# Region attention with a depthwise convolution: index words read four at once, values stored in two DMAs a row, and x, residual and output rows moved by DMAs that POOL begins

## The reference

```
xn = group_norm(x)                      # 32 groups, statistics over a whole image
q, k, v = split(xn @ qkv_w.T + qkv_b)   # 1x1 convolution
q_r, k_r = mean of q, k over each of 7 x 7 regions of 8 x 8 positions
idx = top_k(q_r @ k_r, 4)               # for each of 49 regions the 4 most similar ones
out = softmax(q * 256**-0.5 @ k[idx].T) @ v[idx]   # 8 heads of 32, 64 queries x 256 keys a region
out = out + depthwise_conv3x3(v, lepe_w) + lepe_b
result = x + out @ out_w.T + out_b
```

## Time and profile before

| | us |
|---|---|
| median of 3 runs | 2189.56 (2187.88 to 2190.34) |
| profiled execution, its own time | 2192.58 |
| its span, first to last instruction | 2190.8 |
| PE busy | 1837.4 (84%) |
| DVE busy | 1661.0 (76%) |
| ACT busy | 1623.5 (74%) |
| POOL busy | 617.6 (28%) |
| granted TensorE clock, mean | 0.973 of full |

### The profile page before, as it was taken

How to read it: one execution, slowest core, us unless ns; L and a number is a source line. 1 busy time by engine, 2 the same in 40 slices (tenths; PEclk the granted TensorE clock), 3 DMA queues, 4 the chain that set the end, 5 groups by cost and what they waited for, 6 DMA issues and landing times.

```text
span 2190.8 us, 80869 instructions
## 1 busy us (share of the span) xinstructions
PE 1837.4 (84%) x25672; PEld 1200.2 (55%) x25672; DVE 1661.0 (76%) x3843; ACT 1623.5 (74%) x5017; POOL 617.6 (28%) x1920
## 2 busy tenths in 40 slices
PE   5778888898888888898888998888888988867776
PEld 3345555565555555565556655555555555545444
DVE  4678878788887878788887888878887877766544
ACT  2448878687887787788787878777887877766664
POOL 0013323232332232333232323322323232323222
PEclk9999999999999999999999999999999999998998
DMA  3213333333333333333333333333333333322323
GB/s 108 60 58 89 99 107 99 101 99 111 101 109 95 110 99 107 101 104 101 107 100 105 97 111 101 107 94 109 99 101 92 88 92 92 95 84 83 90 81 86
DMA packets 221330, 212.07 MB, mean 97 GB/s; under 512 B 19328, under 2 KB 220656, under 8 KB 220912
## 3 DMA queue, kind: packets, MB, share of 16 engines
q1 hardware_dynamic: 220912, 206.90, 33.0%
HBM read 155.45 MB, written 51.38 MB: 94 GB/s over the span
## 4 chain that ended last, share of the span: by engine, by line
SPq 69%; issue 15%; PE 8%; DMA 4%; DVE 2%; ACT 1%; POOLq 0%; POOL 0%; DVEq 0%
SPq L242 51%; SPq L210 10%; PE chunk_bank L766 4%; SPq L232 4%; DMA v_sel<-v_dram 2%; DMA v_dram<-v_stage 1%; SPq L254 1%; DVE lepe L522 1%; PE pt_bank L843 1%; SPq L259 1%; PE o_bank L857 1%; PE chunk_bank L779 1%; PE chunk_bank L755 1%; SPq L223 1%; DMA x_in<-x_dram 1%
## 5 line engine op out<-in xcount | busy, mean ns | idle before, releaser
L433 ACT ACTIVATE probs<-s_bank,neg_max 128x256 f32<-128x256 f32 x1568 | 733.6, 476 | 200.4 <-DVE neg_max L626 196.3
L313 POOL COPY k_sel<-k_all 128x128 f32 x1568 | 427.0, 307 | 1048.7 <-PE s_bank L832 1038.4
L626 DVE TENSOR_REDUCE neg_max<-s_bank 128x2 f32<-128x512 f32 x784 | 506.3, 686 | 206.7 <-PE s_bank L832 205.2
L522 DVE SCALAR_TENSOR_TENSOR lepe<-v_band,taps,lepe 128x448 f32<-128x448 f32 x896 | 612.6, 700 | 23.0 <-POOL v_band L329 13.7
L440 ACT COPY probs_t<-pt_bank 128x512 f32<-128x512 f32 x784 | 464.4, 592 | 196.7 <-PE pt_bank L843 193.5
L766 PE MATMUL chunk_bank<-xn,wqkv 128*128 128x448 f32 x1344 | 594.8, 552 | 15.0 <-ACT q_all L416 5.1
L843 PE MATMUL pt_bank<-ident,probs 128*128 128x128 f32 x3136 | 500.8, 283 | 14.3 <-ACT probs_t L440 13.0
L857 PE MATMUL o_bank<-probs_t,v_sel 128*32 128x64 f32 x12544 | 263.9, 226 | 256.9 <-DMA v_sel<-v_dram 256.0
L843 PEld LDWEIGHTS pt_bank<-ident,probs 128*128 128x128 f32 x3136 | 366.7, 143 | 157.3 <-issue 98.1
L857 PEld LDWEIGHTS o_bank<-probs_t,v_sel 128*32 128x32 f32 x12544 | 199.0, 112 | 430.8 <-DMA v_sel<-v_dram 403.1
L433 ACT ACTIVATION_READ_ACCUMULATOR probs<-s_bank,neg_max 128x1 f32 x1568 | 318.9, 203 | 0.0
(11 more groups left out here) (56 smaller groups left out, 1254.2 us busy)
## 6 DMA issues: line engine op xcount, KB each, us to landing
v_sel<-v_dram SPq DMA_DIRECT2D x1568, 64.0 KB
x_in<-x_dram SPq DMA_DIRECT2D x56, 448.0 KB, 3.9
v_dram<-v_stage SPq DMA_DIRECT2D x224, 112.0 KB
resid<-x_dram SPq DMA_DIRECT2D x56, 448.0 KB, 4.0
out_dram<-resid SPq DMA_DIRECT2D x56, 448.0 KB, 3.3
wqkv<-w_qkv_dram SPq DMA_DIRECT2D x1, 768.0 KB, 5.4
wout<-w_out_dram SPq DMA_DIRECT2D x1, 256.0 KB, 6.2
idx_row<-packed_idx SPq DMA_DIRECT2D x8, 0.2 KB
```

The costliest lines, as they stand in the source:

```text
L313: last = pool.tensor_copy(k_sel[:, r % K_SLOTS, :, RT * j:RT * (j + 1)], k_all[:, b % 2, :, bass.ds(reg[j] * RT, RT)])
L433: act.activation(probs[:, u, :], s_bank[:, u, 0:KEYS], ACT.Exp, bias=neg_max[:, r % 2, u:u + 1], accum_out=denom[:, r % 2, u:u + 1]).then_ ...
L522: ins = dve.scalar_tensor_tensor(row, v_band[:, n % BANDS, k, t // 3:t // 3 + RS, t % 3:t % 3 + W], taps[:, k, t:t + 1], row, ALU.mult, AL ...
L626: dve.tensor_reduce(neg_max[:, r % 2, 2 * hf:2 * hf + 2], s_bank[:, 2 * hf:2 * hf + 2, 0:KEYS], AX.X, ALU.max, negate=True).then_inc(max_d ...
```

## The change

- An index row now holds four 32-bit words a region. `chosen` loads all four with one call, and the shifts and masks are gone, on SP and on POOL. DVE no longer packs; the index DMA moves 16 bytes for each of 49 regions.
- v_stage is one buffer over both halves. `store_values(n)` runs once a row, at step 0 of the next s (in the last row of an image at step 6 as before), waits for both halves and begins two DMAs of 224 KB. One semaphore counts them, and `vt_out` waits for it.
- `load_x`, `load_resid` and `store_row` move to POOL's stream: load_x at step 2, store_row at step 4 (it was 3), load_resid at step 5, each behind `gather_keys(r + 2)` and, at steps 0 to 3, `add_bias`.
- `affinity` shares memory with `qk_mean`.

```
-            word = eng.value_load(idx_row[0:1, (r // NREG) % 2, n:n + 1])
-            return [nc.s_assert_within((word >> (IDX_BITS * j)) & (2 ** IDX_BITS - 1), 0, NREG - 1,
-                                       skip_runtime_bounds_check_because="max_index gives one of the 49 regions")
-                    for j in range(TOPK)]
+        def chosen(engine, r):
+            first = TOPK * (r % NREG)
+            return nc.values_load_multi_w_load_instructions(
+                idx_row[0:1, (r // NREG) % 2, first:first + TOPK], engines=[engine], min_val=0, max_val=NREG - 1,
+                skip_runtime_bounds_check_because="max_index gives one of the 49 regions")[1]
...
         @block.sync
-            def store_values(n, m):
+            def store_values(n):
                 b, rr = divmod(n, NWIN)
-                wait_taken(sp, "vt", n, m)
+                for m in range(2):
+                    wait_taken(sp, "vt", n, m)
+                if b >= 2 and rr == 0:
                     sp.wait_ge(attn_done, NREG * (b - 1))
                 for h in range(2):
+                    sp.dma_start(v_dram[b % 2, h:RS:2, rr * W:(rr + 1) * W, :].rearrange("q t d -> t q d"),
+                                 v_stage[PADW * h:PADW * h + W, :, :]).then_inc(v_stored, 16)
...
+                    if rc == 0 and is_row(s + A_LEAD - 1) and rr:
+                        store_values(s + A_LEAD - 1)
...
         @block.gpsimd
...
+            def load_resid(g):
+                if g >= 2:
+                    pool.wait_ge(out_stored[g % 2], 16 * (g // 2))
+                pool.dma_start(resid[:, g % 2, :, :], x_rows[g]).then_inc(resid_in[g % 2], 16)
+
+            def store_row(g):
+                wait_taken(pool, "out", g, 0)
+                wait_taken(pool, "out", g, 1)
+                pool.dma_start(out_rows[g], resid[:, g % 2, :, :]).then_inc(out_stored[g % 2], 16)
+
+            load_x(0)
+            load_x(1)
...
+                    if rc == 2 and 2 <= s + X_LEAD + 2 < ROWS:
+                        load_x(s + X_LEAD + 2)
+                    if rc == 4 and is_row(s - 2):
+                        store_row(s - 2)
+                    if rc == 5 and is_row(s):
+                        load_resid(s)
...
             def choose(b):
-                settle(dve.max_index(top_idx[:], top[:], affinity[:]))
-                for j in range(TOPK - 2, -1, -1):
-                    ins = dve.scalar_tensor_tensor(packed_idx[:, j:j + 1], word, float(2 ** IDX_BITS), ...
+                settle(dve.max(top[:], affinity))
+                dve.max_index(top_idx[:], top[:], affinity).then_inc(top_done, 1)
```

More of the change, by code:

```diff
@@ L7 @@
 U32 = mybir.dt.uint32
-I32 = mybir.dt.int32
 ALU = mybir.AluOpType
@@ L37 @@
 LAST_TAP = KC * (TAPS - 1) - KC
-IDX_BITS = 6
 V_SLOTS = 3
@@ L99, in attention_kernel @@
         v_band = sb("v_band", [P, BANDS, KC, RS + 2, PADW])
-        v_stage = sb("v_stage", [TWO, 2, 2, C])
+        v_stage = sb("v_stage", [TWO, 4, C])
         resid = sb("resid", [TT, 2, NT, C])
@@ L138, in attention_kernel @@
         x_loaded = [sem(f"x_loaded{i}") for i in range(2)]
-        v_stored = [sem(f"v_stored{i}") for i in range(2)]
+        v_stored = sem("v_stored")
         v_sel_in = [sem(f"v_sel_in{i}") for i in range(V_SLOTS)]
@@ L218, in _ @@
         def _(sp):
[L219 to L223, removed]
-            def store_values(n, m):
+            def store_values(n):
                 b, rr = divmod(n, NWIN)
-                wait_taken(sp, "vt", n, m)
-                if b >= 2 and rr == 0 and m == 1:
+                for m in range(2):
+                    wait_taken(sp, "vt", n, m)
+                if b >= 2 and rr == 0:
                     sp.wait_ge(attn_done, NREG * (b - 1))
                 for h in range(2):
-                    first = 4 * m + h
-                    sp.dma_start(v_dram[b % 2, first:first + 3:2, rr * W:(rr + 1) * W, :].rearrange("q t d -> t q d"),
-                                 v_stage[PADW * h:PADW * h + W, m, :, :]).then_inc(v_stored[m], 16)
+                    sp.dma_start(v_dram[b % 2, h:RS:2, rr * W:(rr + 1) * W, :].rearrange("q t d -> t q d"),
+                                 v_stage[PADW * h:PADW * h + W, :, :]).then_inc(v_stored, 16)
             def select_values(r):
-                reg = chosen(sp, r)
+                reg = chosen(mybir.EngineType.SP, r)
                 if r >= V_SLOTS:
@@ L248, in load_index @@
                     sp.wait_ge(k_sel_done, NREG * (b - 1))
[L249 to L261, removed]
+                sp.dma_start(idx_row[:, b % 2, :], top_idx[:, 0:TOPK]).then_inc(idx_in, 16)
             sp.dma_start(ident[:], ident_d).then_inc(weights_in, 16)
@@ L340, in add_bias, with load_x @@
                                    ALU.add).then_inc(resid_ready, 1)
+            def load_x(n):
+                if n >= 2:
+                    wait_full(pool, "x", n - 2, 1)
+                    wait_full(pool, "x", n - 2, 0)
+                pool.dma_start(x_in[:, n % 2, :, :], x_rows[n]).then_inc(x_loaded[n % 2], 16)
+            def load_resid(g):
[8 more added lines that the diff above has]
+            load_x(1)
             pool.memset(neg_half[:], -0.5).then_inc(zeros_done, 1)
@@ L404, in vt_out @@
                 if n:
-                    act.wait_ge(v_stored[m], 32 * n)
+                    act.wait_ge(v_stored, 32 * n)
                 wait_full(act, "vt", n, m)
                 bank = bank_of("vt", n, m)
-                act.copy(v_stage[:, m, :, :].rearrange("p q c -> p (q c)"), bank[0:TWO, :]).then_inc(free("vt", n, m), 1)
+                act.copy(v_stage[:, 2 * m:2 * m + 2, :].rearrange("p q c -> p (q c)"), bank[0:TWO, :]).then_inc(free("vt", n, m), 1)
             def q_out(n, k):
@@ L602, in choose @@
                     dve.wait_ge(idx_in, 16 * b)
-                settle(dve.max(top[:], affinity[:]))
-                settle(dve.max_index(top_idx[:], top[:], affinity[:]))
-                word = top_idx[:, TOPK - 1:TOPK]
-                for j in range(TOPK - 2, -1, -1):
[L607 to L613, removed]
+                settle(dve.max(top[:], affinity))
+                dve.max_index(top_idx[:], top[:], affinity).then_inc(top_done, 1)
             def out_half(g, m):
```

27 lines of the change are left out of this document (6 added, 21 removed).

## The result

| | before | after |
|---|---|---|
| median, us | 2188.72 (4 runs, 2187.83 to 2190.34) | 1942.59 (4 runs, 1938.21 to 1952.65) |
| ratio to before, 95% interval | | 0.888 [0.884, 0.892] |
| profiled execution, its own time | 2192.58 | 1938.21 |
| granted TensorE clock, mean | 0.973 | 0.990 |

The change makes the program 11.2% faster.

The account below looks back on a forecast made before the run. SP's queue was taken to bound the kernel, TensorE afterwards. Seven images save 178 us, the last 12, less 3.6: 186 off 2192.6 gives 2006, as median 2003 us; range 1945 to 2135.

Parts of the forecast that it names:

- in them TensorE stands 0.92 us for DVE's o_norm. I take that once a row: TensorE, four regions behind an image change: their o_norm wait, taken 7 times an image, gives 229.3 us an image.
- 222.8 us an image: TensorE's need without v_sel waits: six images' 1528 us less 191 us of waits, divided by six.
- (a): SP's queue: shifts and masks go, 0.51 us less a region.
- surcharge of 3%: Put on SP's sums because medians summed to 35.3 us a row against 36.4 measured.
- TensorE with DVE behind it is the bound, SP just under it: What is late next: TensorE at 32.7 us a row, above SP's 32.3.
- so nothing is added: Image change: v_sel path from the v_stage copy ends at 668.7, TensorE is ready at 669.2, no loss.
- (b): SP's queue: two stores a row instead of four, 0.95 us less a row.
- (c): SP's queue: x, resid and out leave it, 1.3 us less a row.
- g: POOL's cost to begin one transfer of 448 rows of 1 KB: taken as 1.2 us, three a row.
- Rival 2: POOL late at halo, then DVE, if g exceeds 2.65 us; g = 3.3 gives 2076 us; chance 0.12.
- Rival 3: v_sel lands later beside big transfers in another queue, so the relief comes to nothing: about 2190 us; chance 0.04.
- Rival 4: Less friction: no o_norm wait and a free load, 1949 us; counted within the forecast's range, no separate chance.

Follow-up runs that it names:

- runs with packing kept: DVE's three packing operations put back, unused: in the changed kernel 1945.23 us, 0.889; in the kernel before with only four-word loads 1993.07 us, 0.911.
- two loads of two words: Changed kernel with SP's load of four index words split into two loads of two, all used: 2263.47 us, 1.035.
- moves alone: Kernel before with only the x, residual and output rows begun by POOL: 2158.33 us, 0.987.
- words undone: Changed kernel back to one packed word a region, with shifts and masks on SP and POOL: 2147.66 us, 0.983.
- stores alone: Kernel before with only the values of a row stored by two DMAs in place of four: 2155.84 us, 0.985.
- words alone: Kernel before with only four index words in one load on SP and POOL, no packing: 1989.92 us, 0.909.
- moves undone: Changed kernel with x, residual and output rows begun by SP again: 1963.16 us, 0.897.
- stores undone: Changed kernel back to four stores of values a row: 1985.81 us, 0.908.
- pairs: Changed kernel with SP loading eight index words for two regions at a time: 1907.34 us, 0.872.
- fourth-load kernel: Kernel with eight words a load, and POOL also beginning the fourth load of selected values of a region: 1964.76 us, 0.898.

## Why the prediction was wrong in size

By its own sum the forecast for the profiled execution was 2006 us; it took 1938.2, 68 less.

| us | predicted | measured | difference |
|---|---|---|---|
| first image and the six, 7 times | 1605.1 | 1551.6 | -53.5 |
| last image | 219.5 | 205.7 | -13.8 |
| opening and tail, added | 3.6 | 2.6 | -1.0 |

**The step that failed: "in them TensorE stands 0.92 us for DVE's o_norm. I take that once a row".** It is an event of once an image. In the trace before, six of the seven waits for o_norm in the six images stand at 433, 686, 942, 1198, 1451 and 1707 us (0.60 to 0.92), one behind each image change; the seventh is of 0.38. I turned one wait, in four regions behind a change, into one a row, without asking whether the next row had it. The changed kernel's six images show 2.2 us in four of them, where I had put 42 x 0.92 = 38.6. The runs with packing kept say why it stood there. With it falls the prediction's order of the two: TensorE with DVE behind it was not the bound, SP was.

**The second: 222.8 us an image as TensorE's need.** It is span less wait, and takes for granted that TensorE does the same work in the same busy time once the waits go. It did not. Behind the stall of 3.58 us in the earlier trace rows the clock in the rows is 0.50, that is 1.2 GHz, and at the same place of the changed kernel, behind a stall of 1.44, it is 1.00 or 2.4 GHz. The stretches are the 3.4 us behind an image change, of the kernel before and after, columns as in the earlier trace rows (the clock is the third number from the end):

```profile
673.30:676.70 3.40, 3.40 (x19) 2.77 (x11) 1.79 (x5) 2.20 (x9) 0.00 (x0) 0.50 0.25 66
```

```profile
609.20:612.60 3.40, 3.40 (x49) 2.79 (x49) 2.67 (x7) 2.54 (x12) 1.10 (x2) 1.00 0.47 146
```

Summed over the six images, from the records of granted clock and of matmuls:

| kernel | TensorE busy, us | of the stretch at 1.2 GHz, us | six images, us |
|---|---|---|---|
| two loads of two words | 1352.8 | 119.5 | 1573.8 |
| moves alone | 1338.2 | 87.6 | 1499.5 |
| words undone | 1331.1 | 71.7 | 1486.4 |
| before | 1326.0 | 53.5 | 1528.0 |
| stores alone | 1321.4 | 47.8 | 1495.1 |
| words alone | 1313.0 | 32.2 | 1380.5 |
| moves undone | 1310.0 | 34.1 | 1355.0 |
| stores undone | 1303.6 | 17.7 | 1374.9 |
| after | 1295.7 | 6.2 | 1330.3 |
| pairs | 1293.3 | 2.0 | 1309.0 |

The busy time is, within 6 us, 1293 us plus 0.55 for each microsecond at the lower clock. Only the fourth-load kernel is off it: 1305.6 with none, and there TensorE waits on DVE. So when most of the 191 us of waits went, 30.3 us of busy time went too.

The sum of the waits does not set the time at the lower clock, though. The moves alone have less of them than the kernel before, 148.2 us for 191.0, and more at 1.2 GHz, 87.6 us for 53.5. What they have more of is long single stalls: 39 of over 1.5 us in the six images, for 20 before, 2 after and 1 in the pairs (1.5 is a bound of mine, to count by). Their number alone does not give it either: the moves undone have 6, and 34.1 us.

The six images then close: predicted 1375.6 = 1326.0 busy, 11.0 other idle, 38.6 for o_norm; measured 1330.3 = 1295.7 busy, 11.0 other idle, 23.6 for v_sel. The difference is -30.3 for the busy time, -38.6 for o_norm, +23.6 for the waits I had put at nothing.

**SP's region, 4.48 predicted, 4.20 measured.** (a) held: 4.67 less 0.51 is 4.16. The surcharge of 3%, 0.12 us, had no place on a region read whole from a timeline; it belonged to the row sum only. And e, the price of three more words, is a load behind a v_sel DMA of 0.82 us for 0.79, and 0.319 for 0.288 on POOL: 0.03, where I took 0.2. The two make the last image: 49 x 0.28 = 13.7 of its 13.8 us. A row of SP, summed over all its instructions and the gaps under 0.1 us between them, is 30.8 us where I had 32.3; TensorE's full-clock need is 1293 over 42, 30.8 too. 31.7 us a row came out, 0.9 above either, and the 0.9 is SP's own: beyond its 30.8 it stands 36.5 us in the six images, 25.4 of them at the six image changes and 11.1 in 31 gaps of 0.36 us that the profile puts down to nothing. The prediction's 32.3 names neither; its surcharge, 0.9 a row, happened to stand for them, and in the last image, which has no change of image, there was nothing for it to stand for. Both terms of "TensorE with DVE behind it is the bound, SP just under it" were too large by about the same amount, so mending one of them alone would have moved the forecast little.

The rule in the Trainium skill's "Runtime: NRT & Kernel Launch", section "Instruction fetch mechanics", some 200 ns for each register, does not hold for these loads from on-chip memory: measured are 0.03 us for three more words and 0.23 for four more after those. The prediction also read the median load of 0.63 us as agreeing with a floor of some 600 ns; the earlier trace rows itself has loads of 0.431, and behind an x, resid or out DMA 0.46 was the rule, so no floor of 0.6 shows here.

**The image change, "so nothing is added": roughly right as a path, wrong as a sum.** ACT's copy, SP and TensorE at one of them in the changed kernel:

```profile
597.57 0.60 ACT L401 COPY v_stage<-chunk_bank 114x512 f32<-114x512 f32 x1
```

```profile
598.57 3.31 DMA v_dram<-v_stage
...
601.97 0.47 SPq L207
```

```profile
609.16 0.65 PE L841 MATMUL o_bank<-probs_t,v_sel 128*32 128x64 f32 x32 [1.44 <-DMA v_sel<-v_dram]
...
614.66 0.65 PE L841 MATMUL o_bank<-probs_t,v_sel 128*32 128x64 f32 x32 [0.83 <-DMA v_sel<-v_dram]
```

The copy's end to the attend is 609.16 less 598.17, 11.0 us; I had 10.7. But TensorE is ready at 607.7, 9.6 behind the copy and not 11.2 as before. This is still not where most of TensorE's waits stand. The first attends behind the six changes wait 0 to 3.1 us, 5.3 together, where in the kernel before they waited 2.9 to 7.9. Some 18 of the 23.6 us for v_sel are spread over the rows between, as here, 75 us behind a change:

```profile
1349.01 0.76 PE L841 MATMUL o_bank<-probs_t,v_sel 128*32 128x64 f32 x20 [1.97 <-DMA v_sel<-v_dram]
```

That fits an SP whose row is as long as TensorE's and which has no lead: with the eight words SP gets its lead, and the same waits fall to 5.4 us. What an earlier change would be worth was not tried.

**(b) and (c)** held in size: 112 stores, 0.90 us a row left of 1.96, and nothing of the three big DMAs on SP. SP's row, summed as above, falls from 35.6 to 34.6 us with the stores alone, and to 35.1 with the moves alone, which is 1.3 less what the loads give back. In the kernel with the stores alone TensorE still waits for v_sel in the same manner, with 47.8 us at the lower clock.

**POOL: g = 1.2 us taken, 0.709 measured**, the median in the views of L315, L320 and L325. Rival 2 asked for 2.65 and stayed away: DVE's waits for v_band, at the line of halo that had the most of them, are 5.8 us in 7 times in place of 13.7 in 39. The value is nearer to SP's 0.40 than I took it, and far from the whole way of 3.9. add_bias waited 348.1 us for resid and now 4.0:

```profile
L308 POOL TENSOR_TENSOR resid<-resid,bout 112x256 f32<-112x256 f32 x224 | 165.4, 739 | 4.0 <-DMA resid<-x_dram 4.0
```

No such issue took the 3.1 us that the prediction drew from the page "SBUF — State Buffer" of the Trainium skill, section "SBUF: two separate sides", for a transfer beside a DVE operation in a two-port mode; the longest L320 is 0.90. Rival 3 (v_sel lands later beside the big transfers) is refuted by the waits of 23.6 us. Rival 4, 1949 us by my working, came nearest. It was right that the wait for o_norm goes and that the load's words are nearly free. That its 222.8 us an image lie so near the 221.7 measured is luck: of these TensorE is busy 216 and SP sets the pace. I had put it inside the forecast and yet set the range's lower end at it, as if nothing could go better than "no friction".

## What to carry to other kernels

When one queue is never idle, its row is a plain sum: price it region by region from a timeline, add no surcharge to it, and expect the parts of a change to add. A need worked out as span less waits contains the slow clock that stood beside the waits; read the busy time from a stretch at full clock before you call it the next bound. A queue that never waits for a free buffer still sets the pace, even beside an engine that is 97% busy. A wait found once is an event until the same place of the next row shows it again.

## What the runs showed of the hardware

- The price of reading index words into registers lies almost wholly in the load and in what stands ahead of it, not in the words: 0.46 us behind an x, resid or out DMA, 0.79 behind a v_sel DMA, 0.82 with four words there, 1.05 with eight, 0.47 directly behind another load.
- A DMA of 448 rows of 1 KB takes POOL 0.709 us to begin, against 0.40 on SP, and lands about 1 us later for x: 4.9 us against 3.9; out is at 3.8 against 3.3. The page's part 3 before and with the moves alone shows the same 206.9 MB in far fewer packets, 3.6 KB each in POOL's queue:

```profile
q1 hardware_dynamic: 220912, 206.90, 33.0%
```

```profile
q1 hardware_dynamic: 142960, 129.82, 20.9%
q0 software_dynamic: 21504, 77.08, 12.6%
```

- TensorE's busy time is not a property of the program: the same matmuls of six images took 1293 to 1353 us, in step with the time at 1.2 GHz but for the fourth-load kernel. It is a relation across kernels. No run held everything else fixed, so that the stalls cause the lower clock stays the reading that fits, not one that was isolated.
